# Differential attention with an fp8 feed-forward: scores of two units in a row, quarter-array products beside them, and a rearranged start and end

## The reference, cut to what matters

```python
x = L0_attn_x                                  # (1, 1024, 256) f32
xn = _layernorm(x)
x = x + _L0_attn_ref(xn, ...) + _L0_ffn_ref(xn, ...)

# attention: 16 heads, two sets of queries and keys of 8 columns each, values of 16 columns
q1, k1, q2, k2, v = jnp.split(xn @ Wqkv, [C, 2 * C, 3 * C, 4 * C], axis=-1)   # C = 128
A1 = _causal_sdpa(q1, k1, v)
A2 = _causal_sdpa(q2, k2, v)
diff = A1 - lam * A2                           # lam from four small vectors
diff = diff / jnp.sqrt(jnp.mean(diff * diff, axis=-1, keepdims=True) + EPS)
out = ((1.0 - LAMBDA_INIT) * diff).reshape(...) @ Wproj

# feed-forward in fp8 (E4M3): 256 -> 2 x 1024 -> 256
outputs = _qdot(gelu(_qdot(x, w_gating[0])) * _qdot(x, w_gating[1]), w_linear)
```

## Time and profile before

| what | us |
|---|---|
| median of 3 runs | 193.35 |
| the profiled execution's own time | 192.92 |
| its span, first to last instruction | 191.1 |
| TensorE busy | 182.0 |
| ScalarE busy | 168.1 |
| of it the 96 exps of line 454 | 141.2 |
| VectorE busy | 93.6 |
| GpSimd busy | 59.4 |

### The profile page before, as it was taken

How to read it: one execution, slowest core, us unless ns; L and a number is a source line. 1 busy time by engine, 2 the same in 40 slices (tenths; PEclk the granted TensorE clock), 3 DMA queues, 4 the chain that set the end, 5 groups by cost and what they waited for, 6 DMA issues and landing times.

```text
span 191.1 us, 3572 instructions
## 1 busy us (share of the span) xinstructions
PE 182.0 (95%) x1452; PEld 78.1 (41%) x1452; DVE 93.6 (49%) x220; ACT 168.1 (88%) x146; POOL 59.4 (31%) x71
## 2 busy tenths in 40 slices
PE   6799999799999999999989999999999999999992
PEld 6685344464333323233324334333423434433481
DVE  0975799322223140550274012704750999579852
ACT  2476967999999999999999999999999999999820
POOL 8517600051116321450343053307301630532000
PEclk9999999999999999999999999999999999999999
DMA  5969377780000000000088794000000000000033
GB/s 172 406 254 269 87 193 203 202 193 15 0 0 3 0 0 3 0 0 3 13 199 197 192 194 95 0 0 3 0 0 3 0 3 0 0 0 3 0 113 113
DMA packets 8148, 14.97 MB, mean 78 GB/s; under 512 B 1984, under 2 KB 5312, under 8 KB 8128
## 3 DMA queue, kind: packets, MB, share of 16 engines
q1 hardware_dynamic: 7440, 14.05, 27.3%
q10 hardware_dynamic: 688, 0.66, 1.0%
HBM read 5.26 MB, written 1.05 MB: 33 GB/s over the span
## 4 chain that ended last, share of the span: by engine, by line
PE 58%; ACT 35%; DMA 3%; SPq 1%; DVE 1%; issue 0%
ACT probs L454 35%; PE ps L990 19%; PE ps L978 12%; PE ps L824 9%; PE ps L893 7%; PE ps L830 4%; PE ps L1020 3%; DMA w_q<-L_attn_Wqkv 3%; PE ps L931 1%; PE ps L838 1%; PE ps L814 1%; PE ps L1025 1%; SPq L241 0%; DVE area L581 0%; ACT probs L442 0%
## 5 line engine op out<-in xcount | busy, mean ns | idle before, releaser
L454 ACT ACTIVATE probs<-ps,shift 128x1536 f32<-128x1536 f32 x96 | 141.2, 1540 | 1.6 <-PE ps L978 1.0
L990 PE MATMUL ps<-probs,v_all 128*32 128x512 f32 (+3 forms) x768 | 78.3, 496 | 0.5 <-DVE o_t L654 0.4
L363 POOL TENSOR_SCALAR_AFFINE_SELECT probs<-probs 128x1024 f32<-128x1024 f32 (+1 forms) x40 | 36.7, 917 | 103.9 <-ACT probs L454 103.8
L978 PE MATMUL ps<-q_st,k_st 32*128 32x512 f32 (+3 forms) x384 | 49.9, 420 | 0.4 <-ACT probs L454 0.4
L978 PEld LDWEIGHTS ps<-q_st,k_st 32*128 32x128 f32 x384 | 22.5, 182 | 57.8 <-ACT probs L454 29.9
L654 DVE STREAM_TRANSPOSE o_t<-ps 128x512 f32<-128x512 f32 x16 | 11.5, 717 | 45.4 <-PE ps L990 45.4
L990 PEld LDWEIGHTS ps<-probs,v_all 128*32 128x32 f32 x768 | 16.2, 108 | 19.0 <-issue 13.2
L824 PE MATMUL ps<-xn_t,w_q 128*128 128x256 f32 (+1 forms) x46 | 17.5, 491 | 0.8 <-DMA w_q<-L_attn_Wqkv 0.8
L893 PE MATMUL ps<-area 128*128 128x512 fp8e4 x64 | 14.5, 379 | 0.0
L442 ACT ACTIVATE probs<-ps 128x512 bf16<-128x512 f32 x16 | 9.2, 597 | 3.5 <-PE ps L893 3.0
L581 DVE TENSOR_TENSOR area<-ps,probs 128x512 fp8e4<-128x512 f32 x16 | 10.7, 690 | 1.0 <-ACT probs L442 0.7
(11 more groups left out here) (81 smaller groups left out, 125.2 us busy)
## 6 DMA issues: line engine op xcount, KB each, us to landing
q_st<-parts SPq DMA_DIRECT2D x32, 128.0 KB, 2.8
k_st<-parts SPq DMA_DIRECT2D x32, 128.0 KB, 2.8
probs<-L_ffn_w_gating SPq DMA_DIRECT2D x4, 512.0 KB, 7.8
probs<-L_ffn_w_linear SPq DMA_DIRECT2D x1, 1024.0 KB, 12.0
w_q<-L_attn_Wqkv SPq DMA_DIRECT2D x2, 384.0 KB, 5.8
out<-probs SPq DMA_DIRECT2D x3, 256.0 KB, 2.2
x_sb<-L_attn_x SPq DMA_DIRECT2D x2, 256.0 KB, 4.0
x_sb<-L_attn_x ACTq DMA_DIRECT2D x2, 256.0 KB, 4.3
```

The source lines that it names most:

```text
L363: pool.affine_select(out=blocks, in_=blocks, pattern=pattern, compare_op=ALU.is_ge, fill=0.0, base=0, channel_multiplier=-1).then_inc(mask ...
L454: act.activation(probs[:, at:at + PER_UNIT, :].rearrange("p s u -> p (s u)"), ps[:, 3 * (n % 2):3 * (n % 2) + 3, :].rearrange("p b n -> p ...
L978: ins = pe.matmul(ps[:, bank, at:at + wide * P], k_st[rows, g % STACKS, kb * P:(kb + 1) * P], q_st[rows, g % STACKS, queries], start=True, ...
L990: ins = pe.matmul(ps[32 * j:32 * j + 32, 6, q0 % HALF:q0 % HALF + wide * P], v_all[:, g % HG, kb, 32 * j:32 * j + 32], probs[:, slot + j, ...
```

## The change

Lines of the changed kernel are called L1017 (scores), L1029 (values), L838 (the new quarter products), L854 (values' projection), L1059 (project), L1064 (residual).

1. **Two units in a row.** From unit 2 on TensorE issues scores(n) and scores(n+1), then values due for n, `beside(n)`, `beside(n+1)`, values due for n+1.
2. **Quarters.** `queries_keys` for the second branch, `norms` for it, and the down products are each issued as 4 products on 32 columns of the array (`by_quarters`).
3. **Tables.** `V_AT` puts two blocks beside unit 0, so `QK_AT` begins at 5 and all of `QK_AT` and `NORM_AT` moves up by three to five units; `DOWN_AT` stays. Values' banks are `V_BANK` = 6, 6, 7, 6; `PAIR`'s last eight entries are permuted. VectorE's order of `keep`, `split` and `norm_round` follows, and GpSimd squares unit 7 right behind unit 6.
4. **Wide part first.** Within a unit's scores the wider piece of a chunk comes first.
5. **Start.** x blocks 0 and 2 are loaded singly by SP, 1 and 3 singly by ScalarE's queue, then 4-5 and 6-7 by the latter. `w_q` is loaded as columns 0 to 255 and then 256 to 767.
6. **End.** Blocks 2-3 share bank 0; VectorE adds x to them, so two `residual` products and two copies of ScalarE go.

```diff
-PAIR = [2, 3, 0, 1, 2, 3, 0, 1, 2, 0, 1, 3, 0, 1, 2, 3]
+PAIR = [2, 3, 0, 1, 2, 3, 0, 1, 3, 0, 1, 2, 0, 1, 3, 2]
...
+V_BANK = (6, 6, 7, 6)
...
-V_AT = {0: (2,), 1: (3,), 2: (4,), 3: (5,), 4: (6,), 5: (7,)}
+V_AT = {0: (2, 3), 1: (4,), 2: (5,), 3: (6,), 4: (7,)}
...
-NORM_AT = {23: 0, 31: 1, 39: 2, 41: 3}
+NORM_AT = {19: 0, 27: 1, 35: 2, 37: 3}
...
-            for b in (0, 4):
-                sp.dma_start(x_sb[:, b:b + 2, :], x_rows[:, b:b + 2, :]).then_inc(x_in[b // 2], 16)
-            for k in range(KC):
-                sp.dma_start(w_q[:, k, :], w_qkv[k * P:(k + 1) * P, :]).then_inc(wq_in, 16)
+            for b in (0, 2):
+                sp.dma_start(x_sb[:, b, :], x_rows[:, b, :]).then_inc(x_in[b // 2], 16)
+
+            w_rows = w_qkv.rearrange("(k p) n -> p k n", p=P)
+            sp.dma_start(w_q[:, :, 0:C], w_rows[:, :, 0:C]).then_inc(wq_in, 16)
+            sp.dma_start(w_q[:, :, C:3 * C], w_rows[:, :, C:3 * C]).then_inc(wv_in, 16)
...
-            for b in (2, 6):
+            for b in (1, 3):
+                act.dma_start(x_sb[:, b, :], x_rows[:, b, :]).then_inc(x_in[b // 2], 16)
+            for b in (4, 6):
                 act.dma_start(x_sb[:, b:b + 2, :], x_rows[:, b:b + 2, :]).then_inc(x_in[b // 2], 16)
...
-            dve.wait_ge(y_ready, 4)
-            dve.tensor_tensor(y[:, 4:6, :].rearrange("p b c -> p (b c)"), ps[:, Y_BANK[4], :],
-                              x_sb[:, 4:6, :].rearrange("p b c -> p (b c)"), ALU.add).then_inc(y_added, 1)
-            dve.wait_ge(y_ready, 6)
+            for b in (2, 4):
+                dve.wait_ge(y_ready, b // 2 + 1)
+                dve.tensor_tensor(y[:, b:b + 2, :].rearrange("p b c -> p (b c)"), ps[:, Y_BANK[b], :],
+                                  x_sb[:, b:b + 2, :].rearrange("p b c -> p (b c)"), ALU.add).then_inc(y_added, 1)
+            dve.wait_ge(y_ready, 5)
...
+            def by_quarters(bank, at, left, right, start, stop):
+
+                for q in range(0, P, 32):
+                    ins = pe.matmul(ps[q:q + 32, bank, at:at + right.shape[-1]], left[:, q:q + 32], right, start=start,
+                                    stop=stop, skip_group_check=True)
+                return ins
...
                     for c in range(first, end):
-                        ins = pe.matmul(ps[:, 7, (b % 2) * C:(b % 2 + 1) * C], hidden[:, c, b * P:(b + 1) * P],
-                                        w_lin8[:, c, :], start=(c == 0), stop=(c == HC - 1))
+                        ins = by_quarters(7, (b % 2) * C, hidden[:, c, b * P:(b + 1) * P], w_lin8[:, c, :],
+                                          c == 0, c == HC - 1)
...
-                for n in range(n0, n0 + BRANCH):
+                first = HG if general and br == 1 else 0
+                if br == 0:
+                    for n in range(2):
+                        scores(n, general)
+                        beside(n)
+
+                for n in range(2 if br == 0 else n0, n0 + BRANCH, 2):
                     scores(n, general)
-                    values_due(n, HG if general and br == 1 else 0, GROUPS)
+                    scores(n + 1, general)
+                    values_due(n, first, GROUPS)
                     beside(n)
...
+                    beside(n + 1)
+                    values_due(n + 1, first, GROUPS)
...
-                pe.wait_ge(res_ready, TB // 2)
-                for b in (2, 3):
-                    project(b, 0, start=True)
-                    residual(b)
-                    project(b, 1).then_inc(y_ready, 1)
+                project(2, 0, start=True)
+                project(3, 0)
+                project(2, 1)
+                project(3, 1).then_inc(y_ready, 1)
...
```

More of the change, by code:

```diff
@@ L85, in last_unit, with wide_first @@
     return (chunk * J + J - 1) // PER_UNIT
+def wide_first(c):
+    return sorted(range(len(CHUNKS[c])), key=lambda p: -CHUNKS[c][p][1])
 def due(g, c):
@@ L459, in whole @@
             def whole(b):
-                act.wait_ge(y_ready, (1, 1, 2, 3, 4, 4, 5)[b])
+                act.wait_ge(y_ready, 4 if b == 6 else 1)
                 at = C if b == 1 else 0
@@ L466, in _ @@
             act.activation(newton[:, 1, 112:113], newton[:, 0, 0:1], ACT.Sqrt)
-            for b in (0, 1, 2):
+            for b in (0, 1):
                 whole(b)
@@ L470, in _ @@
             act.activation(newton[:, 3, 112:128], newton[:, 0, 112:128], ACT.Sqrt).then_inc(rms_ready, 1)
-            for b in (3, 6):
-                whole(b)
-            act.wait_ge(y_copied, 5)
+            whole(6)
+            act.wait_ge(y_copied, 3)
             act.dma_start(out_rows[:, 6, :], y[:, 6, :]).then_inc(y_out, 16)
@@ L519, in stats_of @@
                 for b in range(2 * i, 2 * i + 2):
-                    dve.wait_ge(x_in[b // 2], 16)
+                    dve.wait_ge(x_in[b // 2], 32 if b < 4 else 16)
                     own.mark(dve.bn_stats(stats[:, b, :], x_sb[:, b, :]))
@@ L731, in _ @@
             keep(0, 1)
-            keep(1, 0)
             split(5)
             norm_round(0)
-            keep(1, 1)
+            keep(1, 0)
             split(6)
             norm_round(1)
+            keep(1, 1)
             keep(2, 0)
@@ L740, in _ @@
             norm_round(2)
-            keep(2, 1)
             norm_round(3)
@@ L749, in _ @@
             bound1.bias()
+            keep(2, 1)
             keep(3, 0)
@@ L819, in _ @@
                 pe.matmul(ps[:, 7, 0:P], ident[:, :], ident[:, :], start=True, stop=True)
+            def by_quarters(bank, at, left, right, start, stop):
[3 more added lines that the diff above has]
+                return ins
             def queries_keys(u, bank, k, at, wide):
                 i, h = QK_UNITS[u]
+                if i >= 2:
+                    return by_quarters(bank, at, w_q[:, k, i * P:(i + 1) * P],
+                                       xn_t[:, k, h * HALF + at:h * HALF + at + wide], k == 0 and at == 0, k == KC - 1)
                 return pe.matmul(ps[:, bank, at:at + wide], w_q[:, k, i * P:(i + 1) * P],
@@ L864, in _ @@
             transposes(2)
+            pe.wait_ge(wv_in, 16)
             project_values(0, 6)
@@ L922, in beside @@
                     norms(4 + r, 7).then_inc(round_ready, 1)
+                if n == REST_AT:
+                    pe.wait_ge(ffn_out, TB // 2)
+                    pe.wait_ge(res_ready, 1)
+                    residual(0, start=True)
+                    residual(1)
+                if n == Y_AT:
+                    pe.wait_ge(wp_in, 16 * 8)
+                    pe.wait_ge(out_t_ready, 2)
+                    project(0, 0)
+                    project(1, 0)
                 if n in DOWN_AT:
@@ L970, in scores @@
                 items = [((PER_UNIT * u + e) // J, (PER_UNIT * u + e) % J, 3 * (n % 2) + e) for e in range(PER_UNIT)]
-                for p in range(2):
+                for turn in range(2):
                     for c, j, bank in items:
-                        if p == len(CHUNKS[c]):
+                        if turn == len(CHUNKS[c]):
                             continue
+                        p = wide_first(c)[turn]
                         kb, wide, q0 = CHUNKS[c][p]
@@ L1000, in values @@
                 (kb, wide, q0), *more = CHUNKS[c]
-                if g == 0 and c < 2:
-                    pe.wait_ge(v_out, (6, TB)[c])
+                if g == 0 and c == 0:
+                    pe.wait_ge(v_out, TB)
                 if c == 0 and g > 0:
@@ L1017, in project @@
             def project(b, p, start=False):
-                at = b % 2 * C if b in (0, 1, 4, 5) else 0
+                at = b % 2 * C if b < 6 else 0
                 return pe.matmul(ps[:, Y_BANK[b], at:at + C], out_t[:, p, b * P:(b + 1) * P], w_p[:, p, :],
```

53 lines of the change are left out of this document (24 added, 29 removed).

## The result

| | us | runs |
|---|---|---|
| before | 193.34 (193.13 to 193.37) | 4 |
| changed | 196.27 (195.50 to 197.59) | 4 |
| ratio | 1.0161, 95% interval 1.0100 to 1.0222 | |

Slower by 1.6% where 0.4% was forecast, and 0.4 us beyond the range. The four runs of the changed kernel are 195.50 and 195.78 at a mean granted clock of 1.000, 196.76 at 0.991 and 197.59 at 0.983; the profile is of the last. So part of the loss stands in every run and part comes with the clock. Medians and ranges are of all runs, while the ratios and their intervals leave out runs over 1.5% above the fastest of their kernel: three of e9, one each of e10 and e14, and one run of before at 929.59 us.

The account below looks back on a forecast made before the run. The prediction took the exps, 1.43 us apart with TensorE as slow as ScalarE, to bound the kernel. 192.92 + 1.45 (exps) - 0.4 (start) - 0.3 (end) = 193.67 profiled; the median 0.43 above, 194.1 us, range 192.0 to 195.9.

Parts of the forecast that it names:

- What bounds the kernel: Exp stage: exps 1.43 us apart at best, TensorE as slow as ScalarE; rearrangement could give back at most 5.4 us.
- No lead from pair to pair: Every pair starts at an exp's end, so TensorE carries no lead onward; an ordinary pair is late by 0.14 us.
- the even units named: Pairs 64-65 and 74-75, with two value products and a down product between: exps 66 and 76 late, 2.0 us together.
- the four other heavy pairs: Pairs 82-83 and 86-87 (0.34 us each), 90-91 (0.26) and 78-79 (0.3 to 0.4): 1.35 us late together.
- The norms: Pairs at 19, 27 and 35 that carry a norm: late by 0.5, 0.35 and 0.25 us, together 1.1.
- The sixteen small late exps: Ordinary pairs, chunk 2 halves and early value projections: 16 exps late by 0.1 to 0.26 us, together 2.4.
- the ordinary pairs: Pairs with two products beside: late by 0.14 us, falling due at every other pair.
- Quarters: Products on 32 columns priced as value products; a fp8 down step stays at 0.107 us, upper bound 1.9 us over 64 steps.
- the third rival: Quarters don't run four abreast in fp8 or 2 bytes: 1.9 us more in late pairs, 196.0 us; chance 0.15.
- The first rival: Saved changes of kind count and ordinary pairs never fall late: 2.4 us less, 191.7 us; chance 0.2.
- Start: Single x blocks and split `w_q`: first statistics earlier, passed on in full to the first projection; 0.4 us gained.
- End: Two fewer TensorE products gain 0.46 us until VectorE's transpose limits; exp 95 slips 0.15; net gain 0.3.

Follow-up runs that it names:

- e9: Kernel of e5 with the scores of units 39, 40, 62, 63, 86 and 87 waiting for one exp more; 196.06 us.
- e10: Kernel of e5 with 10 instead of 14 warm-up products; 189.80 us.
- e14: Kernel of e5 with only the scores of unit 63 waiting for one exp more; 189.52 us.
- e4: Changed kernel with the old loads: x blocks in twos and `w_q` whole, on the old queues; 194.89 us.
- e11: Kernel before with the new end alone; 192.26 us.
- e5: Changed kernel with units one at a time and the old loads of x and `w_q`; 188.07 us, best of the study.
- e1: Changed kernel with units one at a time in the old order; 188.74 us.
- e3: Kernel before with the quarter products alone; 190.83 us.
- e2: Kernel before with the pair order alone, on the old tables; 198.98 us.
- e7: Changed kernel with the down products of units 64 and 75 moved to 61 and 72; 194.64 us.
- e8: Changed kernel with four identity products between scores 62 and 63, and units 90 and 91 one at a time; 196.10 us.
- e12: Changed kernel with four identity products between scores 62 and 63, and two projections moved from unit 87 to 93; 196.10 us.
- e13: As e12, but with the two projections beside unit 91; 195.53 us.

## Why the prediction was wrong in size

The direction and the main mechanism were right: the pairs take away TensorE's lead, and the exps come late at the units named. What failed are terms of the sum. Beside each, what the runs showed:

| term | forecast | measured |
|---|---|---|
| exps, clock at 1.000 | +1.45 | +2.5 (e4) |
| start | -0.4 | +0.4 (first exp) |
| end | -0.3 | -0.8 (e11) |
| falls of the clock | no term | +0.6 in the median |

The median lies 2.2 us above the forecast (196.27 and 194.1). The exps (1.05), the start (0.8, with the wrong sign) and the clock (0.6) are 2.45 of it, the end takes back 0.5, and some 0.2 stays without a term. Step by step:

- **What bounds the kernel: right.** All versions differ by how late the exps come. e5 has them at 137.4, near the floor of 135.9.
- **No lead from pair to pair: right, and it carries the loss.** Late exps come at the even units named: exp 66 late by 1.15 and 76 by 1.03 (e4) for a forecast of 2.0 together, the four other heavy pairs 1.54 for 1.35. The norms are 1.1 for 1.1, but that is partly luck: 0.66, 0.34 and 0.08 for 0.5, 0.35 and 0.25. e1 against the changed kernel shows that the pairs alone turn 2.2% faster into 1.6% slower.
- **The sixteen small late exps: too small.** Forecast 2.4 together, in e4 3.2, and it is sixteen exps there too. The step that failed is "Between the halves 0.98 passes today (136.35 to 137.33); two quarter pieces cover 0.86, so 0.12 is added". The 0.98 begins behind a change of kind, which quarters take away. What is fixed is the time from the start of one half to that of the other, set by VectorE's take: 1.55 before (135.78 to 137.33 in its timeline) and 1.55 now, and 1.48 to 1.55 in seven of the eight groups of the changed kernel. So the saved change brings nothing, and 0.23 is added. Timeline of PE of the changed kernel, units 8 and 9:

```profile
48.65 0.64 PE L1029 MATMUL ps<-probs,v_all 128*32 128x256 f32 x8
49.11 1.05 PE L838 MATMUL ps<-xn_t,w_q 128*32 128x256 f32 x16
50.20 0.64 PE L1029 MATMUL ps<-probs,v_all 128*32 128x256 f32 x8
```

In e4 exp 10 is late by 0.39, exps 32 and 34 by 0.40 together, 44 and 46 by 0.40, exp 58 by 0.34, each for a forecast of 0.26. That is some 0.5 of the missing 0.8; the rest is spread over the ordinary pairs, 0.13 to 0.18 each for 0.14, and is not traced further. The exps of e4 take 145.3 from the first start to the last end, for 144.2 forecast: +2.5 where I had +1.45.
- **The granted clock: no term for it.** Two falls cost the exps 1.25 and 1.35 us in the changed kernel's profile, and the median of its runs lies 0.6 above its two runs at 1.000. I took the earlier trace rows, a clock of 1.00 throughout, as given, and my own forecast of TensorE waiting at every pair should have raised the question.
- **Quarters: right.** 0.107 a fp8 step kept (273 ns four abreast for 274), the third rival is out. That its 196.0 lies next to the measured 196.27 is chance.
- **The first rival had half of it.** Saved changes of kind do count: 2.1 us in e3, and e1 is 3.8 us of exps faster than before, 1.7 of it by the moved tables and the wide part first, which I priced at 0 and which were not split. With pairs the same parts are still worth 2.4 (146.2 in e2, 143.8 in e4). But the ordinary pairs fall late all the same, and the pairs cost 5.0 to 6.4.
- **Start: wrong sign.** The step that failed is "I take 0.4. It passes on." The first statistics did come 0.76 sooner. But TensorE was at its 14 warm-up products until about 7.1, so transposes began at 6.97; and blocks 4-5 and 6-7, now last on ScalarE's queue, were read only at 7.67 and 10.63, which ends in the wait at 15.62 and made the first exp 0.38 later. In the other profiles with the new loads it came 0.44 to 0.93 later than e5's (e1, e7, e8, e12, e13). Their last chains go through the same late loads: x blocks in e8, e12 and e13, the fp8 weights in e1 and e7, whose casts begin at 15.77 in e1, 2.3 later than before. Against the forecast that is 0.8, and e5 against e1, on two chips, is 0.7 us in the medians. Not all of it is the loads: e2, with the old ones, had its first exp at 36.56, because its warm-up products ended at 7.92.
- **End: right, a little too small.** 0.54 measured at the last issue for 0.46, 0.83 in the medians of e11, where the rest isn't traced.

The sum again, for a run without falls: +2.5 by the exps, +0.4 by the start, -0.8 by the end is +2.1, and 195.50 and 195.78 less 193.34 is +2.3. The falls make it +2.9. Left open is why some gaps are followed by a fall and others of the same length are not.
